# Attention on one NeuronCore: score and maximum matmuls over 32 rows of one head instead of 128 rows of a spread key tile

## The reference

```python
k = (x @ Wk).reshape(b, t, h, s); q = ...; v = ...      # 16 heads of 8 numbers
k = _layernorm(k, kln_w, kln_b); q = _layernorm(q, qln_w, qln_b)
dot = jnp.einsum('bqhs,bkhs->bhqk', q, k) * scale
dot = jnp.where(causal, dot, -jnp.inf)
attn = jax.nn.softmax(dot, axis=-1)
out = jnp.einsum('bhqk,bkhs->bqhs', attn, v).reshape(b, t, e)
return out @ Wo + bo
```

## Time and profile before

| | |
|---|---|
| median of three executions | 2882.5 us (2881.77 to 2883.07) |
| span of the profiled execution | 2834.4 us |
| what lies around the span, against the median | 48.1 us |
| attention stage within the span | about 17 to 740 us |
| busy over the whole span | PE 93%, PEld 60%, DVE 63%, ACT 56%, POOL 29% |
| mean granted TensorE clock | 0.969 |

### The profile page before, as it was taken

How to read it: one execution, slowest core, us unless ns; L and a number is a source line. 1 busy time by engine, 2 the same in 40 slices (tenths; PEclk the granted TensorE clock), 3 DMA queues, 4 the chain that set the end, 5 groups by cost and what they waited for, 6 DMA issues and landing times. The chain is left out here.

```text
span 2834.4 us, 54508 instructions
## 1 busy us (share of the span) xinstructions
PE 2635.7 (93%) x19182; PEld 1713.2 (60%) x19182; DVE 1789.9 (63%) x3491; ACT 1578.4 (56%) x2843; POOL 820.0 (29%) x1181
## 2 busy tenths in 40 slices
PE   5999998998689979999999999999999999996997
PEld 3555565655478845666555665555555555554886
DVE  7777777786466745555665556555556655555666
ACT  2666666666454455555555556555566555554443
POOL 4142422525345311111111111112121123322642
PEclk8999999999799979999999999999999999997998
DMA  6500000001424258888878888887888788885222
GB/s 109 82 16 16 8 16 16 16 9 31 119 83 157 94 130 196 195 196 196 204 184 200 196 196 189 190 187 177 188 189 190 183 201 200 206 199 203 71 87 85
DMA packets 190430, 383.21 MB, mean 135 GB/s; under 512 B 45281, under 2 KB 100714, under 8 KB 188810
## 3 DMA queue, kind: packets, MB, share of 16 engines
q1 hardware_dynamic: 181578, 362.55, 53.9%
q0 software_dynamic: 8640, 17.84, 1.8%
HBM read 38.10 MB, written 39.86 MB: 28 GB/s over the span
## 5 line engine op out<-in xcount | busy, mean ns | idle before, releaser
L3050 DVE STREAM_TRANSPOSE m_turned<-m_sig 128x1024 f32<-128x1024 f32 x512 | 613.6, 1227 | 429.5 <-ACT m_sig L2820 201.1
L2643 PE MATMUL m_v_ps<-m_sig,m_tok 128*64 128x512 f32 x2048 | 468.2, 599 | 0.0
L2656 PE MATMUL m_v_ps<-m_sigT,m_tok 128*64 128x256 f32 x4064 | 461.5, 380 | 3.2 <-DMA m_sigT<-m_turned 3.2
L1208 DVE TENSOR_REDUCE a_maxima<-a_bank 128x1 f32<-128x512 f32 (+4 forms) x624 | 367.4, 643 | 121.1 <-PE a_bank L707 73.2
L2627 PE MATMUL m_f_ps<-m_swap,m_own 64*128 64x512 f32 x1536 | 426.2, 404 | 15.6 <-DMA m_swap<-m_own 7.4
L894 ACT ACTIVATE a_prob<-a_bank 128x512 f32<-128x512 f32 (+1 forms) x608 | 322.2, 586 | 201.0 <-PE a_bank L719 197.5
L2627 PE MATMUL m_f_ps<-m_own,m_swap 64*128 64x512 f32 x1536 | 426.4, 404 | 0.0
L2656 PEld LDWEIGHTS m_v_ps<-m_sigT,m_tok 128*64 128x64 f32 x4064 | 289.4, 137 | 200.3 <-issue 54.8
L2916 POOL TENSOR_TENSOR m_own<-m_uv,m_own 128x1024 fp32r<-128x1024 f32 x64 | 152.0, 2375 | 813.4 <-ACT m_own L2782 813.4
L2820 ACT ACTIVATE m_sig<-m_f_ps 128x1024 f32<-128x1024 f32 x256 | 248.3, 1022 | 245.4 <-issue 147.5
L2627 PEld LDWEIGHTS m_f_ps<-m_swap,m_own 64*128 64x128 f32 x1536 | 271.6, 186 | 99.9 <-ACT m_sig L2806 25.8
(11 more groups left out here) (509 smaller groups left out, 4268.6 us busy)
## 6 DMA issues: line engine op xcount, KB each, us to landing
m_sigT<-m_turned SPq DMA_DIRECT2D x2042, 128.0 KB, 2.3
m_swap<-m_own SPq DMA_DIRECT2D x64, 256.0 KB, 3.2
f_t_rows<-f_sent_rows SPq DMA_DIRECT2D x142, 65.0 KB, 2.1
f_sent_rows<-a_proj SPq DMA_DIRECT2D x34, 260.0 KB, 9.5
k_apart<-a_kT SPq DMA_DIRECT2D x64, 128.0 KB, 2.4
m_swap<-m_own SPq DMA_DIRECT2D x64, 128.0 KB, 3.2
f_h<-back_rows SPq DMA_DIRECT2D x8, 512.0 KB, 5.6
rows<-back_rows SPq DMA_DIRECT2D x6, 512.0 KB, 4.9
```

Source lines behind the costliest of these rows:

```text
L1208: dve.tensor_reduce(maxima[:, qt, h:h + heads, part], src, AX.X, ALU.max).then_inc(u.free(), 1)
L2643: mm = pe.matmul(v2_ps[h * RANK:(h + 1) * RANK, :], tok[p][:, 0, j + s * SIDE, :], sig[j % 2][s][:, h * HALF:(h + 1) * HALF], start=(j == ...
L2656: mm = pe.matmul(v1_ps[h * RANK:(h + 1) * RANK, g * 2 * P:(g + 1) * 2 * P], tok[p][:, 1, jj, :], sigT[g][:, :, 2 * h:2 * h + 2, jj, :].rea ...
L3050: dve.transpose(turned[g][:, :, q, :, :], sig[j % 2][s][:, :].rearrange("p (t j a) -> p j t a", j=4, a=STACK)).then_inc(turn_ready, 1)
```

## The change

Scores and maxima no longer read `k_apart`. They read 32 partitions of `kT` and of `qT` or `qmT`: the rows of one head. The two tiles, their clearing and the copying DMAs are gone. A unit is now always one head: 40 score units and 40 maximum units, in which consecutive units of a kind belong to different heads, and the maxima's heads run two ahead of the scores'. Some units hold two pieces (two tiles of queries, or of keys), the mask is one 128-wide matmul per diagonal piece: 32 per group instead of 23 of several widths. Keys have three buffers; keys and queries are turned two groups ahead, and ScalarE empties them and `turn_high`. The maxima run from score unit 0 to 37.

```diff
-            pool.memset(k["k_apart0"][:, :, :].bitcast(F32), 0.0)
...
-    SCORE_UNITS, MAX_UNITS = 38, 39
+    SCORE_UNITS, MAX_UNITS = 40, 40
...
+    KEPT_KEYS = 3
...
+        SCORE_PIECES = (((0, 0, HALF),), ((1, P, HALF),), ((0, HALF, SEQ),), ((1, HALF, SEQ),), ((2, 2 * P, HALF), (3, 3 * P, HALF)),
+                        ((2, HALF, SEQ),), ((3, HALF, SEQ),), ((4, 4 * P, SEQ),), ((5, 5 * P, SEQ),), ((6, 6 * P, SEQ), (7, 7 * P, SEQ)))
+        MAX_PIECES = (((0, 0, P), (1, 0, 2 * P)), ((2, 0, 3 * P),), ((3, 0, HALF),), ((4, 0, HALF),), ((5, 0, HALF),),
+                      ((4, HALF, 5 * P), (5, HALF, 6 * P)), ((6, 0, HALF),), ((6, HALF, 7 * P),), ((7, 0, HALF),), ((7, HALF, SEQ),))
+        SCORES = [(pieces, h) for pieces in SCORE_PIECES for h in range(GROUP)]
+        MAXES = [(pieces, (h + GROUP // 2) % GROUP) for pieces in MAX_PIECES for h in range(GROUP)]
...
-            keys_ahead = prep or g < HALVES_OF
-            begin, end, made = PLACE[4], 36, 0
-            if prev and follows:
-                yield "spread", 0
+            two_ahead, first = prep or g < HALVES_OF, follows and not prev
+            begin, end, made = 6 if first else 0, 37, 0
...
+                if two_ahead and i in (31, 32, 34, 35):
+                    yield ("keys", "queries")[i // 34], (31, 32, 34, 35).index(i) % HALVES_OF
...
-                for h in range(GROUP):
-                    rows = head_rows(h)
-                    sp.dma_start(k_apart[g % 2][rows, h, :].bitcast(F32), kT[g % 2][rows, :].bitcast(F32)).then_inc(k_spread, 16)
...
-                if n == 0:
-
-                    pe.wait_ge(k_spread, 16 * GROUP * (G + 1))
-                for i in range(heads):
-                    mm = pe.matmul(out[:, i, :], qT[g % 2][:, qt * P:(qt + 1) * P], k_apart[g % 2][:, h + i, k0:k1], start=(i == 0 or not masked), stop=not masked)
-                if masked:
-                    mask = k["mask"][:, :].unsqueeze(1).broadcast_to([P, heads, P])
-                    mm = pe.matmul(out[:, :, k1 - k0 - P:k1 - k0], k["ident16"][:, :], mask, start=False, stop=True)
+                for qt, k0, k1 in pieces:
+                    masked = k1 == (qt + 1) * P
+                    mm = pe.matmul(out[:, col:col + k1 - k0], qT[G % 2][rows, qt * P:(qt + 1) * P], kT[G % KEPT_KEYS][rows, k0:k1],
+                                   start=True, stop=not masked)
+                    col += k1 - k0
+                    if masked:
+                        mm = pe.matmul(out[:, col - P:col], k["ident16"][:, :], k["mask"][:, :], start=False, stop=True)
...
-                    mm = pe.matmul(out[:, i, :], k_apart[g % 2][:, h + i, j * P:(j + 1) * P], qmT[g % 2][:, q0:q1], start=True, stop=True)
+                for j, q0, q1 in pieces:
+                    mm = pe.matmul(out[:, col:col + q1 - q0], kT[G % KEPT_KEYS][rows, j * P:(j + 1) * P], qmT[G % 2][rows, q0:q1], start=True, stop=True)
+                    col += q1 - q0
...
+                    elif what == "keys":
+                        empty(u, half_of(kT[(G + 2) % KEPT_KEYS], n))
+                    elif what == "queries":
+                        empty(u, half_of(qT[g % 2], n))
+                    elif what == "turn_high":
+                        empty(u, half_of(qmT[g % 2], 1))
...
-            pool.memset(k["k_apart1"][:, :, :].bitcast(F32), 0.0).then_inc(other_cleared, 1)
...
+                for qt, k0, k1 in pieces:
+                    width = k1 - k0
+                    to = first_max[:, qt % HALF_T, h:h + 1] if k0 else maxima[:, qt, h:h + 1]
+                    ins = dve.tensor_reduce(to, src[:, col:col + width], AX.X, ALU.max)
...
-                    elif what == "turn_high":
-                        keep_turned(u, half_of(qmT[g % 2], 1))
```

More of the change, by code:

```diff
@@ L425, in score_units @@
[L425 to L438, removed]
@@ L500, in sequence @@
                     yield "stack_queries", 3
[L501 to L517, removed]
+                if first and i in (1, 3):
+                    for n in range(HALVES_OF):
+                        yield ("next_keys", "next_queries")[i // 2], n
+                if prev and i == 3:
+                    yield "turn_high", 0
+                if prev and i == 5:
+                    for n in WEIGHED_LATE:
+                        yield "weigh", n
+                if prev and i == 9:
+                    yield "empty_out", 0
+                if two_ahead and i in (31, 32, 34, 35):
+                    yield ("keys", "queries")[i // 34], (31, 32, 34, 35).index(i) % HALVES_OF
                 if follows and begin <= i <= end:
@@ new lines, in sequence @@
+                if prep and g == 2 and i in (0, 2, 5, 7, 9, 10, 12, 20, 21):
+                    yield {0: ("square", 1), 2: ("square", 0), 5: ("square_sums", 0), 7: ("head_dev", 0), 9: ("head_rstd", 0),
+                           10: ("affine", 1), 12: ("stack_keys", 0), 20: ("affine", 0), 21: ("stack_queries", 0)}[i]
+                if prep and g in (3, 0) and prev and i == 12:
+                    for what in ("stack_keys", "stack_queries"):
+                        yield what, (g + 2) % GROUPS
@@ L890, in weights @@
             def weights(u, n):
-                j, h, heads, q0, q1 = SCORES[n]
-                src = by_head(u.next(), q1 - q0, heads)
+                pieces, h = SCORES[n]
+                src, width = u.next(), sum(q1 - q0 for _, q0, q1 in pieces)
+                to, off = prob_of(*pieces[0][0:2])
+                start = pieces[0][1] - off
                 u.wait_full(act)
-                act.activation(prob[j % 2][:, h:h + heads, prob_cols(j, q0, q1)], src, ACT.Exp).then_inc(u.free(), 1)
+                act.activation(to[:, h, start:start + width], src[:, 0:width], ACT.Exp).then_inc(u.free(), 1)
             def empty_out(G):
@@ L1411, in group @@
                         out_stats(b - 1, n)
-                    elif what in ("score", "keys", "turn_low", "turn_tokens", "turn_z", "project"):
+                    elif what in ("score", "keys", "queries", "turn_low", "turn_high", "turn_tokens", "turn_z", "project"):
                         u.next()
```

208 lines of the change are left out of this document (79 added, 129 removed).

## The result

The changed kernel takes 3150.14 us (median of four, 3140.11 to 3157.45) against 2882.14 for the kernel before; the ratio is 1.0931 [1.0903, 1.0959]. It is slower by 268 us, where 32 us of gain were forecast.

The account below looks back on a forecast made before the run. TensorE was taken as the bound, VectorE close behind. Fourteen windows at -2.0 us (-28) and the start at -3.9 make -32 us: span 2802, plus 48.1, gives 2850.5 us, range 2815 to 2900.

Parts of the forecast that it names:

- Rival B: Attention windows: quarter-row matmuls lower the granted clock, mean 0.97 to 0.85, total 2917 us; sign: below 0.93; chance 0.12.
- Changing the shape of the array: TensorE, plain group: 86 changes between 32-row and 128-row matmuls against 14 before, 0.10 us each, range 0 to 0.2.
- Unmasked pairs: Score and unmasked maximum run together, 0.23 us a pair instead of 0.46; 16 in a group, -3.7 us.
- rival A: Entering or leaving the 32-row shape costs more than 0.10 us; at 0.2, 2930 us in total; chance 0.13.
- Singly masked pairs: Score, maximum and one mask cost 0.48 us instead of 0.59; 16 pairs in a group, -1.8 us.
- Small tiles: Query tiles 0 and 1 and the tails of 4 and 5: doubly masked units, 0.86 us beside a score; +2.4 us a group.
- Waits: TensorE's waits for the spread DMAs go, -0.1 us a group; half those for `turn_high`, -0.35.
- Rivals C and D: C: ring stays full, only the start won, 2879 us, chance 0.13. D: four matmuls at a time, 2822 us, chance 0.14.
- The start: Opening: no clearing of `k_apart0` (-3.1 us), no wait for the spread (-2.8), some 2.0 given back; sum -3.9 us.
- The last term: The 48.1 us by which the median lay above the span before, added to the predicted span of 2802 us.
- Nothing behind the attention stage is touched: Everything after the attention stage: claimed untouched by the change, with no term in the sum.

Follow-up runs that it names:

- order_128rows_late: Changed kernel with the earlier kernel's 128-row operands, keys spread by transfers, maxima from unit 7 of a group: 2878.19 us, 1.0003 of the kernel before.
- mask_32rows_apart: Changed kernel with each triangle added by four 32-row matmuls and the maxima's heads one, not two, ahead: 2937.11 us, 1.0199 of the kernel before.
- heads_apart: Changed kernel with the maxima's heads one further than the score's instead of two: 3089.61 us, 1.0672 of the kernel before.
- pad_128rows: Changed kernel with one added 512-column matmul over 128 rows ahead of each score unit: 3393.30 us, 1.1765 of the kernel before.
- start_only: Kernel before with only the clearing of `k_apart0` moved behind GpSimd's opening work: 2872.21 us, 0.9977 of the kernel before.

## Why the prediction was wrong

**The step that failed is the granted clock.** The sum took all 14 windows at the clock of before. Rival B named the mechanism and the place, with a chance of 0.12, and sized it at a mean of 0.85; it was 0.68, far below the 0.93 that the prediction had set as the sign of B. The other step, *Changing the shape of the array* and *Unmasked pairs*, failed too, by less when it is priced at full clock. Against order_128rows_late (the same order over 128 rows, 613.7 us for 15 windows), exponential by exponential, the changed kernel's 300 us at 2.4 GHz cover 277, and its 539 at 1.2 GHz cover 335. Had the factor 300/277 held throughout, the 15 windows would have taken some 51 us more than 613.7; the remaining 175 of the 231 us are the clock's, and 5 are the order's. This split depends on which step is mended first. mask_32rows_apart takes out most changes of shape and the pairs in one row group, still with 32 rows and a clock of 0.80, and its windows take 671.06 us: that alone gives back 169 of the 231 us. The two steps multiply, a change costs more at half clock and fewer changes leave the clock higher, and the 128 rows of order_128rows_late mend both.

- *Unmasked pairs*: matmuls of two row groups start within 0.03, as forecast, but two of them cost 0.33, not 0.23; the 64-row rows of the message stage were no measure for it. And "score and maximum stand two heads apart" is true of the table and false of the sequence from unit 19 on. Where no mask stands between, neighbours of one kind then run side by side instead (401.50); where one does, score and maximum stand one after the other. heads_apart prices that at 61 us.
- *Changing the shape*: mask to score took 0.16, as forecast. A 384-wide maximum to its mask took 0.26; from 32 rows to a 16-bit matmul over 128 took 0.33 where it was 512 wide (a padded unit of pad_128rows), as forecast too. Between 32-bit matmuls it is 0.20 a change rather than 0.10, the upper end of the range, rival A's price.
- *Singly masked pairs*: 0.59 with heads apart, 0.76 in one row group (0.60 + 0.16), instead of 0.48, and that with a maximum of 384 columns where the earlier trace rows have 512: no gain or a loss. *Small tiles*: 1.12 instead of 0.86 for a unit beside a score.
- *Waits*: PE's waits for the spread and for `turn_high` are gone, as forecast, and are worth nothing while PE itself is the bound and slower. Rivals C and D fell: the ring is seldom full (from 115 to 980 us PE waited 8.5 us for DVE to empty a bank), and where three 32-row scores overlap, the matmuls behind them still follow at 0.33.
- *The start*: right for the clearing, wrong for the rest. L90 takes 0.34 (0.2 was stated) and the first maximum starts at 36.49 (near 36 was); alone, the clearing's part is 0.9977. But the term took 2.0 us for the opening's units and clock together, and with the 32-row operands the first copy comes 27.5 us later than before (0.54 mean clock from 100.00 to 142.80 us); in order_128rows_late it comes at 116.27.
- *The last term*: the 48.1 us around the span belong to the chip, not to the kernel; the forecast of 32 us less does not rest on them.
- *Nothing behind the attention stage is touched*: right within the scatter. From the last copy to the end it is 2155.8 us here, 2141 to 2160 in the other kernels where before takes some 2880 us.

What stays open: what exactly, beside rows in use, decides when the clock is taken back; the experiments move a mean, and no run isolates it. And why the clock stays down for whole groups: at 1.2 GHz the same work is spread thinner over time still, which would keep it there, but no run tested that.

## What to carry to other kernels

Spreading a 32-row operand over 128 rows of zeros looks like waste, and here it bought the clock: the zeros cost no time (0.23 us for 512 columns in the earlier trace rows, 0.33 for as many over 32 rows), and at 32 rows the kernel ran at 1.2 GHz for 64% of the 15 windows. Before packing matmuls into row groups, ask whether they will really run side by side all the time (other row group, no 128-row matmul between), or the array works thinner than before; even with most of that mended, mask_32rows_apart had a clock of 0.80 and was slower than 128 rows by 2%. And read the granted clock by stretch before any count of busy time: a PE that is busy 100% can be at half speed.

## What the runs showed of the hardware

- The granted clock falls with TensorE busy throughout (0.62 in 58.48 of 58.48 us), and comes back when more full-row matmuls are added to those of pad_128rows and nothing else (0.68 to 0.96).
- Added work can cost almost nothing: 640 matmuls of 512 columns over 32 rows, ratio 1.0931 to 1.0895; 1280 more over 128 rows, 1.1765 to 1.1858.
- 32-row matmuls of different row groups start together, even three at a time, but 512 columns of float32 then occupy 0.33 us at 2.4 GHz before the next start, against 0.23 for one over 128 rows.
- Two chips of the kind differ by 1.7% on the same kernel (2833.65 and 2883.82 us), nearly all of it behind the attention stage: from the last copy of `o_acc` to the end it is 2110.1 us in the trace of before and 2148.0 in that of start_only, which changes the start alone.
